# Block-diagonal k by DMA and patches turned by transposing DMAs, in a vision tower on one core

## The chip, the cores and the metric

The kernel runs on one core of one Trainium2 chip. A core has five engines that work through instruction streams of their own, in order: PE (TensorE, matmuls and transposes into the PSUM memory), DVE (VectorE), ACT (ScalarE), POOL (GpSimd) and SP (SyncE, which here only issues DMAs). They share the on-chip memory SBUF and wait for each other through semaphores. The metric is the device time of one execution in microseconds (us), the median of three runs.

## What is computed

Sixty-four images of 3 x 112 x 112 are cut into 49 patches of 768 values. With a class token in front each image has L = 50 tokens of 256 values.

```python
xn = _rms_norm(patches)
xq = _act_quant(xn)                     # 8-bit integers times a scale, per patch
h = concat([cls, xq @ wq.T], axis=1) + pos_embedding
for i in range(3):                      # three attentions; with 50 tokens all windows see the same tokens
    q, k, v = (proj(W, b) for W, b in ((Wq[i], bq[i]), (Wk[i], bk[i]), (Wv[i], bv[i])))   # 16 heads of 16
    scores = einsum('bhqd,bhkd->bhqk', q, k) * 4, causal
    w = e / (sum(e) + 1e-06)            # e = exp(scores - max)
    out_i = layer_norm(einsum('bhqk,bhkd->bhqd', w, v) @ Wo[i].T + bo[i])
h = h + layer_norm(concat(out_i) @ Wout.T + bout)      # input of the attentions: layernorm(h)
h = h + ffn(layernorm(h))               # quantized to 8 bits: silu(x @ Wg.T) * (x @ Wu.T), then @ Wd.T; width 704
```

## The kernel before

The 64 images go in eight groups (m) of eight; two images, 64 rows apart, make a pair that fills the 128 partitions, so a group has four pairs (p) and the kernel 32 pairs (n). The first program block does patches and attention for all groups, the second the feed-forward part. In the first, each engine walks its own list of steps. The table `AT` gives each step's places in its engine's list, sorted by `engine_order`; a step is a kind, a number within the group and the group. The lists of neighbouring groups are interleaved. So the order of the work is written out as numbers, and semaphores only keep it right.

The steps that matter here, per pair: "sums" (SP loads x_in, ACT and DVE gather the row statistics), "shift" (ACT scales into x_t, L733; DVE rounds into the bf16 buffer x_q, L1083), "turn_q" (PE turns x_q by six transposes of 128 columns into a PSUM bank, L1287; ACT copies the bank to x_qT, L746, or for a chunk of the feed-forward weights, which pass through the same steps as a ninth group, to wgT, L743), "embed" (PE multiplies x_qT by the token weights, L1296; DVE finishes the row, L1104), "norm_x" and "turn_x". Of x_t, x_q and x_qT there is one buffer each: DVE writes the next x_q when the last one has been turned and copied out.

Per group follow q and k for each of the three windows w and the two halves c of the 256 dimensions ("k" and "q": six matmuls each on PE, L1314; ACT evicts them to kT, L766, and qT), v (L1333), and then scores per step s (six in a group: window and half of the images). A score matmul (L1358) takes 64 partitions, the 16 dimensions of four heads, so k must stand block-diagonally in k_bd: for each head its own 16 rows, zeros elsewhere. Before the change POOL writes k_bd in "spread": it multiplies kT, repeated four times, by a mask of rows (L905, two operations of 128x400 per pair and window, 192 in all). k_bd has four slots of one pair each, so POOL waits until the scores of the slot's last user are through. After the scores: maximum and exponent ("max", "soft", "sum", "over" on DVE, ACT), POOL normalizes (L914), PE turns the probabilities ("turn_p", L1373), ACT copies them to pT (L806, L813), PE multiplies by v ("heads", L1383) and by the output weights ("project", L1394 and L1399), DVE accumulates.

All PE results except scores go through four PSUM banks in turn; `bank_plan` deals them out in the order of PE's list, and a step waits until its bank's last user has been evicted (`wait_released`). "fold" (L1253) and other set-up steps prepare weights during group 0.

Of the kernel before, what the change touches and what calls it, by code (L numbers as in the profile page):

```python
# [69 lines left out]
        "sums": (0, 1, 5, 6, 7, 8, 9, 10, 11, 12, 13, 14, 15, 16, 17, 18, 19, 20, 21, 22, 23, 24, 25, 26, 27, 28, 29,  # L70
            30, 31, 32, 33, 34, 35, 36, 37, 38, 39, 40,),
        "weights": (2, 3, 4,),
    },
    "act": {
        "sums": (0, 1, 10, 11, 25, 26, 51, 54, 99, 100, 117, 125, 176, 178, 195, 200, 250, 256, 268, 278, 324, 326,
            342, 346, 401, 402, 429, 439, 481, 482, 501, 504,),
        "shift": (2, 5, 13, 15, 33, 39, 61, 71, 106, 113, 137, 145, 185, 188, 205, 213, 260, 266, 283, 289, 332, 338,
            356, 362, 407, 419, 451, 466, 490, 495, 511, 528, 563, 568, 595, 618,),
        "tok_shift": (3,),
        "turn_q": (4, 9, 16, 19, 43, 55, 69, 82, 110, 129, 140, 156, 189, 209, 221, 232, 265, 277, 292, 298, 337,  # L80
            358, 367, 376, 421, 445, 460, 471, 496, 508, 527, 538, 577, 593, 611, 635,),
        "tok_copy": (6, 7,),
        "q_hi": (8,),
        "k_hi": (12,),
        "v_cut": (14, 18, 36,),
        "small": (17,),
        "wv_hi": (20,),
        "turn_x": (21, 22, 23, 24, 93, 95, 97, 98, 170, 171, 172, 173, 244, 246, 247, 248, 319, 321, 322, 323, 397,
# [1709 lines left out]
```

## Time and profile before

| | us |
|---|---|
| runs shown: median (lowest to highest) | 771.42 (769.8 to 774.2) |
| the profiled execution | 769.84 |
| its span, first to last instruction | 768.1 |
| PE busy | 684.5 (89%) |
| DVE busy | 641.9 (84%) |
| ACT busy | 584.3 (76%) |
| POOL busy | 520.0 (68%) |
| mean granted TensorE clock | 0.975 |

The span is the profiled execution's; 1.7 us lie around it. Busy time is the union of an engine's instructions; PE's matmuls overlap each other in the records, so a matmul's own duration is longer than its distance to the next. What a block of matmuls costs PE is read as the distance from its first start to the next block's first start. A timeline row gives start, length, engine, line, operation, and in brackets the engine's idle time ahead of it and what ended it.

### The profile page before, as it was taken

To read this page: it belongs to the slowest core of one execution; us is meant where nothing else is said; L and a number is where in the kernel's file an instruction comes from. 1 tells how busy PE (TensorE), PEld (TensorE's weight loads), DVE (VectorE), ACT (ScalarE), POOL (GpSimd) and SP (SyncE) were. 2 spreads that over 40 slices of the span, in tenths; PEclk is the share of its full clock that TensorE was granted. 3 is DMA by queue.
4 is the path that set the end of the run, shared out by engine and by line. 5 is a ranking of instruction groups with operands and counts; after the bars stand their busy time and mean duration, and the time that the engine had idled before them with its cause. 6 is when DMAs were issued, how large, how long until landed. Compare 5 with 4: busy or idle time off the path is not lost. (4 is left out here: it accounts for less than half of the span.)

```text
span 768.1 us, 25770 instructions
## 1 busy us (share of the span) xinstructions
PE 684.5 (89%) x9862; PEld 535.2 (70%) x9862; DVE 641.9 (84%) x1395; ACT 584.3 (76%) x1280; POOL 520.0 (68%) x793
## 2 busy tenths in 40 slices
PE   0498799999999999999999999999999999568866
PEld 0277678777877787877877787788778777334455
DVE  4788876899889988989898899889987898759947
ACT  3567888687788678869778878688868887379875
POOL 3459965957687859877677789478948786521154
PEclk9979999999999999999999999999999999869979
DMA  8301000000000000101000000100100000000005
GB/s 240 100 28 33 17 19 17 19 18 20 4 32 27 10 2 34 34 2 33 18 19 3 16 19 3 34 18 18 41 3 22 20 22 22 1 1 1 0 24 148
DMA packets 14980, 21.95 MB, mean 29 GB/s; under 512 B 1992, under 2 KB 11466, under 8 KB 14860
## 3 DMA queue, kind: packets, MB, share of 16 engines
q1 hardware_dynamic: 14424, 19.91, 8.4%
q8 instruction: 80, 1.31, 0.7%
q10 hardware_dynamic: 436, 0.40, 0.4%
q14 instruction: 40, 0.33, 0.1%
HBM read 17.03 MB, written 3.28 MB: 26 GB/s over the span
## 5 line engine op out<-in xcount | busy, mean ns | idle before, releaser
L905 POOL TENSOR_TENSOR k_bd<-kT,rmask 128x400 f32<-128x400 f32 x192 | 167.8, 902 | 7.5 <-PE ps_s L1358 4.3
L806 ACT COPY pT<-ps_w 25x400 f32<-25x400 f32 x192 | 94.8, 494 | 9.2 <-PE ps_w L1373 6.7
L1399 PE MATMUL ps_w<-oy_hi,o_hi 128*128 128x512 f32 x192 | 94.9, 494 | 0.0
L914 POOL TENSOR_TENSOR prob_hi<-prob_hi,rsum 128x800 f32<-128x800 f32 x48 | 74.9, 1559 | 13.3 <-DVE rsum L1151 13.3
L1134 DVE TENSOR_REDUCE nmax<-ps_s 128x16 f32<-128x400 f32 x96 | 72.4, 765 | 11.6 <-PE ps_s L1358 11.3
L786 ACT COPY v_bd<-ps_w 50x256 f32<-50x256 f32 x192 | 70.4, 367 | 13.2 <-PE ps_w L1333 10.9
L1399 PE MATMUL ps_w<-oy_hi,o_lo 128*128 128x512 f32 x192 | 76.3, 397 | 0.0
L1399 PE MATMUL ps_w<-oy_lo,o_hi 128*128 128x512 f32 x192 | 76.2, 397 | 0.0
L827 ACT ACTIVATE ps_w<-ps_w 128x256 f32<-128x256 f32 x96 | 35.6, 371 | 51.7 <-PE ps_w L1399 50.3
L1358 PE MATMUL ps_s<-k_bd,qT 64*25 64x200 f32 (+1 forms) x3072 | 70.5, 291 | 0.0
L919 POOL TENSOR_TENSOR ln<-ln,ln_eps 128x1 f32<-128x1 f32 x96 | 19.9, 208 | 74.6 <-ACT ps_w L827 74.1
L1314 PE MATMUL ps_w<-xh_dense,qk_hi 128*128 128x400 f32 x192 | 68.5, 357 | 1.5 <-DVE xl L1126 1.1
L1314 PE MATMUL ps_w<-xl,qk_hi 128*128 128x400 f32 x192 | 67.2, 350 | 0.0
L1314 PE MATMUL ps_w<-xh_dense,qk_lo 128*128 128x400 f32 x192 | 66.2, 345 | 0.0
L1333 PE MATMUL ps_w<-wv_hi,xh 128*128 128x256 f32 x192 | 61.9, 322 | 0.0
L921 POOL TENSOR_TENSOR ln<-ln,neg_half 128x1 f32<-128x1 f32 x96 | 54.4, 567 | 7.5
L914 POOL TENSOR_TENSOR prob_lo<-prob_lo,rsum 128x400 f32<-128x400 f32 x48 | 42.5, 886 | 19.5 <-DVE rsum L1151 19.5
L1373 PE MATMUL ps_w<-pack,prob_hi 128*128 128x128 f32 x384 | 51.7, 277 | 2.9 <-DVE acc L1169 1.0
L1333 PE MATMUL ps_w<-wv_lo,xh 128*128 128x256 f32 x192 | 54.0, 281 | 0.0
L1333 PE MATMUL ps_w<-wv_hi,xl 128*128 128x256 f32 x192 | 53.7, 280 | 0.0
L1373 PEld LDWEIGHTS ps_w<-pack,prob_hi 128*128 128x128 f32 x384 | 42.1, 141 | 11.1 <-issue 6.5
L813 ACT COPY pT<-ps_w 128x400 f32<-128x400 f32 x96 | 43.3, 506 | 8.1 <-PE ps_w L1373 7.3
(237 smaller groups left out, 2070.4 us busy)
## 6 DMA issues: line engine op xcount, KB each, us to landing
x_in<-in_x SPq DMA_DIRECT2D x64, 147.0 KB
out<-hidden SPq DMA_DIRECT2D x14, 200.0 KB
pT<-in_tok_w SPq DMA_DIRECT2D x1, 768.0 KB, 6.5
hidden<-in_wq SPq DMA_DIRECT2D x1, 768.0 KB, 8.6
k_bd<-in_wk SPq DMA_DIRECT2D x1, 768.0 KB, 9.5
v_bd<-in_wv SPq DMA_DIRECT2D x1, 768.0 KB, 9.2
hidden<-in_wout SPq DMA_DIRECT2D x1, 768.0 KB, 9.3
hidden<-in_wo SPq DMA_DIRECT2D x1, 768.0 KB, 10.8
```

Of the source, the lines that this page charges most:

```text
L786: last = nc.scalar.copy(v_bd[row:row + L, s % 2, b::2, :, e * HD:(e + 1) * HD], v_ps[src:src + L, :, e])
L806: last = nc.scalar.copy(pT[ROWB * h:ROWB * h + LQ, s % 2, c::2, :, 0:LQ], ps_w[row:row + LQ, bank].rearrange("p (j t) -> p j t", j=4)[:, : ...
L813: nc.scalar.copy(pT[:, s % 2, 4 * a:4 * a + 4, :, LQ:L], ps_w[:, bank].rearrange("p (j t) -> p j t", j=4)[:, :, 0:QB * LQ].rearrange("p j ...
L905: last = nc.gpsimd.tensor_tensor(k_bd[:, v % KBD, c], kT[:, w % 2, c, 2 * p * L:(2 * p + 2) * L].unsqueeze(1).broadcast_to([P, HR, 2 * L]) ...
L914: nc.gpsimd.tensor_tensor(pr, pr, rsum[:, s % 2, e].unsqueeze(2).broadcast_to([P, H, WIDTH[e]]), ALU.mult).then_inc(prob_ready, 1)
L921: nc.gpsimd.tensor_tensor(ln2[:, v, 2:3], ln2[:, v, 1:2], neg_half[:, 0:1], ALU.pow).then_inc(r2_ready, 1)
L1134: nc.vector.tensor_reduce(top, s_ps, AX.X, ALU.max, negate=True).then_inc(max_ready, 1)
L1314: mm = nc.tensor.matmul(G[:, 0:GT], wt[:, w, q, k, c * P:(c + 1) * P], xt[:, k, :, 0:L], start=(t == 0), stop=(t == 3 * KC - 1))
L1333: mm = nc.tensor.matmul(cols, xt[:, k, two].rearrange("p b t -> p (b t)"), wt[:, w, k], start=False, stop=(k == KC - 1 and xt is xl))
L1358: mm = nc.tensor.matmul(ps_s[32 * b:32 * b + LQ, e, r, c * HR * W:(c + 1) * HR * W], qT[rows, w % 2, c, first:first + LQ], k_bd[rows, v % ...
L1373: mm = nc.tensor.transpose(G[:, j * P:(j + 1) * P], flat[:, (4 * a + j) * P:(4 * a + j + 1) * P], pack[:])
L1399: mm = nc.tensor.matmul(G[:], ot[:, s % 2, c, 2 * (p % 2):2 * (p % 2) + 2].rearrange("p b t -> p (b t)"), wt[:, w, c], start=False, stop=( ...
```

## The change

Three things change.

First, k_bd is no longer computed by POOL but written by DMAs. The columns of the q and k weights are put into another order as they are split into high and low parts (`by_dim`, `in_dims`), so that partition 4i + h of a half holds dimension i of head h. Head h's rows are then every fourth partition, and the step "kbd" on SP copies them by one DMA per head, four per step s, from kT (now ordered by pair) into k_bd. The zeros are written once, by "kclear" on POOL. The scores wait for the landing (`kbd_landed`). The mask rmask goes, and the biases of q and k are loaded in the new order by sixteen DMAs ("biases") in place of two.

Second, from the second group on, and for the four weight chunks of gate and up, the patches are turned by the step "turn_d" on SP: six transposing DMAs of 128 x 128 from x_q to x_qT (or wgT). It waits for x_q and for the embed of the pair before; embed and the next x_q wait for its landing. PE's six transposes and ACT's copy stay for group 0 alone.

Third, the numbers in `AT` are new for all five engines; SP's list grows from 41 to 122 steps.

```diff
+        "kbd": (10, 11, 14, 15, 20, 23, 24, 25, 30, 31, 33, 34, 38, 39, 43, 44, 47, 48, 52, 53, 57, 58, 60, 65, 66,
...
+        "turn_d": (12, 17, 18, 21, 27, 29, 32, 36, 40, 45, 46, 50, 54, 59, 61, 62, 70, 73, 74, 79, 82, 83, 89, 90,
...
+        "turn_q": (5, 9, 17, 18,),
...
-    kT = sb(att, "kT", [P, 2, KC, GT])
+    kT = sb(att, "kT", [P, 2, PAIRS, KC, 2 * L])
...
-    SMALL = 16 * 12
+    SMALL = 16 * 9
...
+
+    def by_dim(t):
+        return t.rearrange("p (s k) (a h i) -> p s (k a) i h", k=KC, h=HR, i=HD)
+
+    def in_dims(t):
+        return t.rearrange("p s k (a i h) -> p s (k a) i h", h=HR, i=HD)
...
+                if kind == "turn_d":
+                    n = PAIRS + step[1]
+                    c = ffn_chunk(n // PAIRS, n % PAIRS)
+                    sp.wait_ge(xq_ready, n + 1)
+                    if c is None:
+                        bank, fill = bank_of(("embed", (n - 1) % PAIRS, (n - 1) // PAIRS))
+                        sp.wait_ge(filled[bank], fill)
+                        dst = x_qT[:]
+                    else:
+                        dst = wgT[:, c // 2, 3 * (c % 2):3 * (c % 2) + 3].rearrange("p f k t -> p (f k) t")
+                    for j in range(PC):
+                        sp.dma_start(dst[:, j], x_q[:, j * P:(j + 1) * P], transpose=True).then_inc(xqT_turned, 16)
                 if kind == "weights" and step[1] == 0:
-                    for dst, src in ((mask_st, mask), (hmask, head_mask), (qbias[:], bq), (kbias[:], bk), (gcol, ln_g),
+                    for dst, src in ((mask_st, mask), (gcol, ln_g),
...
+                if kind == "biases":
+                    for dst, src in ((qbias, bq), (kbias, bk)):
+                        for a in (0, 1):
+                            for h in range(HR):
+                                row = a * ROWB + h * HD
+                                sp.dma_start(dst[a * ROWB + h:(a + 1) * ROWB:HR], src[row:row + HD]).then_inc(loads["bias"], 16)
+                if kind == "kbd":
+                    s = step[1]
+                    w, q = s // 2, s % 2
+                    sp.wait_ge(k_ready, KC * (NS * m + w) + 2)
+                    if m == 0 and s == 0:
+                        sp.wait_ge(kbd_clear, 1)
+                    need(sp, scores_ready, (U * m + 2 * (s - 1) + AHEAD) if m > 0 or s > 1 else 0)
+                    for h in range(HR):
+                        sp.dma_start(k_bd[h::HR, 2 * q:2 * q + 2, :, h, :],
+                                     kT[h::HR, w % 2, 2 * q:2 * q + 2]).then_inc(kbd_landed[q], 16)
...
+            sp.wait_ge(xqT_turned, 16 * PC * PAIRS * GROUPS)
...
+                    act.wait_ge(loads["bias"], 16 * 16)
...
-                    nc.scalar.copy(qk_hi[:, :, 0], by_row(st_q)).then_inc(split_q, 1)
+                    nc.scalar.copy(in_dims(qk_hi[:, :, 0]), by_dim(st_q)).then_inc(split_q, 1)
...
-                    c = ffn_chunk(m, p)
-                    if c is not None:
-                        w_ps = ps_w[:, bank, 0:PC * P // 2].bitcast(BF16)
-                        dst = wgT[:, c // 2, 3 * (c % 2):3 * (c % 2) + 3].rearrange("p f k t -> p (f k t)")
-                        nc.scalar.copy(dst, w_ps).then_inc(xqT_ready, 1)
-                        return
...
-
-                    act.wait_ge(kbd_ready, V * m + (0, -PAIRS, PAIRS)[w] + AHEAD)
-                    nc.scalar.activation(kT[:, w % 2, c], ps_w[:, bank, 0:GT], ACT.Identity,
+                    for landed in kbd_landed:
+                        need(act, landed, 64 * (NS * m + (0, -1, 1)[w]))
+                    nc.scalar.activation(kT[:, w % 2, :, c], ps_w[:, bank, 0:GT].rearrange("p (v t) -> p v t", v=PAIRS), ACT.Identity,
                                          bias=kbias[:, w * KC + c:w * KC + c + 1]).then_inc(k_ready, 1)
...
+                if kind == "kclear":
+                    nc.gpsimd.memset(k_bd[:], 0.0).then_inc(kbd_clear, 1)
...
-                if kind == "spread":
-                    v = step[1]
-                    w, p = v // PAIRS, v % PAIRS
-                    pool.wait_ge(k_ready, KC * (NS * m + w) + 2)
-                    pool.wait_ge(consts, 1)
-                    pool.wait_ge(small_ready, 1)
-                    pool.wait_ge(scores_ready, U * m + 2 * ((v - KBD) // 2 + 1) + AHEAD)
-                    for c in range(KC):
-                        last = nc.gpsimd.tensor_tensor(
-                            k_bd[:, v % KBD, c], kT[:, w % 2, c, 2 * p * L:(2 * p + 2) * L].unsqueeze(1).broadcast_to([P, HR, 2 * L]),
-                            rmask[:].unsqueeze(2).broadcast_to([P, HR, 2 * L]), ALU.mult)
-                    last.then_inc(kbd_ready, 1)
...
-                    nc.vector.tensor_tensor(qk_lo[:, :, 0], by_row(st_q), qk_hi[:, :, 0].bitcast(F32), ALU.subtract).then_inc(qk_cut, 1)
+                    nc.vector.tensor_tensor(in_dims(qk_lo[:, :, 0]), by_dim(st_q), in_dims(qk_hi[:, :, 0]).bitcast(F32),
+                                            ALU.subtract).then_inc(qk_cut, 1)
...
-                    need(dve, xqT_ready, n)
+                    need(dve, xqT_ready, min(n, PAIRS))
+                    need(dve, xqT_turned, 16 * PC * (n - PAIRS))
                     nc.vector.tensor_scalar(x_q[:], x_t[:], MAGIC, None, ALU.subtract).then_inc(xq_ready, 1)
...
-                    pe.wait_ge(xqT_ready, PAIRS * m + p + 1)
+                    if m == 0:
+                        pe.wait_ge(xqT_ready, p + 1)
+                    else:
+                        pe.wait_ge(xqT_turned, 16 * PC * (PAIRS * (m - 1) + p + 1))
...
-                    pe.wait_ge(kbd_ready, V * m + 2 * s + 2 + AHEAD)
+                    pe.wait_ge(kbd_landed[q], 64 * (NS * m + w + 1))
```

PE in group 1, around the embeds of its first two pairs (tokT,x_qT); `ps_w<-hidden` are the folds of the output weights, `id,x_q` the transposes, `pack` the turned probabilities. Before:

```order
L1373 MATMUL ps_w<-pack,prob_lo 128x128 x4
L1296 MATMUL ps_w<-tokT,x_qT 128x256 x6
L1287 MATMUL ps_w<-id,x_q 128x128 x6
L1349 MATMUL ps_s<-mask,pick 128x200 x2
L1358 MATMUL ps_s<-k_bd,qT 25x100 x16
L1349 MATMUL ps_s<-mask,pick 128x8x25 x2
L1358 MATMUL ps_s<-k_bd,qT 25x200 x16
L1243 MATMUL ps_w<-id,hidden 128x128 x4
L1253 MATMUL ps_w<-hidden 128x256 x4
L1373 MATMUL ps_w<-pack,prob_hi 128x128 x8
L1243 MATMUL ps_w<-id,hidden 128x128 x4
L1296 MATMUL ps_w<-tokT,x_qT 128x256 x6
```

and after the change:

```order
L1320 MATMUL ps_w<-tokT,x_qT 128x256 x6
L1274 MATMUL ps_w<-hidden 128x256 x12
L1320 MATMUL ps_w<-tokT,x_qT 128x256 x6
L1397 MATMUL ps_w<-pack,prob_lo 128x128 x4
L1354 MATMUL ps_w<-bias,ones 128x256
```

The transposes between the embeds are gone, and the three folds alone stand between the two. (Each fold of the listing's x4 shows as x8 in the profile's records.)

PE in group 2 of the changed kernel, from its first pair's embed to its second's; `mask,pick` and `k_bd,qT` are scores, `pT,v_bd` heads:

```order
L1320 MATMUL ps_w<-tokT,x_qT 128x256 x6
L1397 MATMUL ps_w<-pack,prob_lo 128x128 x4
L1373 MATMUL ps_s<-mask,pick 128x200 x2
L1382 MATMUL ps_s<-k_bd,qT 25x100 x16
L1407 MATMUL ps_w<-pT,v_bd 32x50 x32
L1373 MATMUL ps_s<-mask,pick 128x8x25 x2
L1382 MATMUL ps_s<-k_bd,qT 25x200 x16
L1397 MATMUL ps_w<-pack,prob_hi 128x128 x8
L1320 MATMUL ps_w<-tokT,x_qT 128x256 x6
```

and around the first of these two embeds before the change:

```order
L1383 MATMUL ps_w<-pT,v_bd 32x50 x32
L1349 MATMUL ps_s<-mask,pick 128x200 x2
L1358 MATMUL ps_s<-k_bd,qT 25x100 x16
L1349 MATMUL ps_s<-mask,pick 128x8x25 x2
L1358 MATMUL ps_s<-k_bd,qT 25x200 x16
L1296 MATMUL ps_w<-tokT,x_qT 128x256 x6
L1373 MATMUL ps_w<-pack,prob_lo 128x128 x4
L1314 MATMUL ps_w<-xh_dense,qk_hi 128x400
```

The embeds of one group have moved closer to each other here: before, q and k matmuls, a transposing block and more stand between the two.

SP after the biases; before the change only the loads of x stand here:

```order
L616 DMA acc<-in_brow 1x1024
L631 DMA x_in<-in_x 49x768 x60
L628 DMA x_in<-in_w_gate 128x2x256
```

and after it:

```order
L640 DMA kbias<-in_bk 16x6 x8
L665 DMA x_in<-in_x 49x768 x4
L649 DMA k_bd<-kT 32x4x100 x8
L621 DMA_TRANSPOSE x_qT<-x_q 128x128 x6
L665 DMA x_in<-in_x 49x768 x2
L649 DMA k_bd<-kT 32x4x100 x8
L665 DMA x_in<-in_x 49x768 x2
L621 DMA_TRANSPOSE x_qT<-x_q 128x128 x12
```

SP's queue now holds three kinds of DMAs behind each other, each with a wait of its own in front.

## Rows read from the trace of the kernel before

**Rows 1.** The page's first part: busy us of each engine, share of span, instructions.
```profile
PE 684.5 (89%) x9862; PEld 535.2 (70%) x9862; DVE 641.9 (84%) x1395; ACT 584.3 (76%) x1280; POOL 520.0 (68%) x793
```

**Rows 2.** Table of windows: from:to, length, busy us per engine, PEclk, DMA share, GB/s.
```profile
40.00:80.00 40.00, 36.68 (x388) 29.15 (x386) 33.12 (x64) 29.52 (x56) 32.17 (x37) 0.92 0.08 24
80.00:640.00 560.00, 544.18 (x8660) 438.27 (x8658) 488.17 (x1103) 447.10 (x1023) 424.79 (x662) 1.00 0.06 19
```

**Rows 3.** Timeline of POOL, then of ACT: start us, us, what, [idle before, releaser].
```profile
53.60 9.89 POOL L905 TENSOR_TENSOR k_bd<-kT,rmask 128x400 f32<-128x400 f32 x8 [0.90 <-ACT kT L766]
...
63.58 0.60 ACT L766 ACTIVATE kT<-ps_w,kbias 128x400 f32<-128x400 f32 x1 [3.67 <-POOL k_bd L905]
```

**Rows 4.** Timeline of PE in the tail: the last attention heads.
```profile
658.58 0.92 PE L1383 MATMUL ps_w<-pT,v_bd 128*32 128x50 f32 x64 [2.27 <-ACT pT L813]
```

**Rows 5.** Timeline of PE around two blocks of turned patches (L1287).
```profile
62.06 0.49 PE L1287 MATMUL ps_w<-id,x_q 128*128 128x128 bf16 x6 [0.83 <-issue]
62.37 0.43 PE L1314 MATMUL ps_w<-xh_dense,qk_hi 128*128 128x400 f32 x1
...
63.56 0.28 PE L1330 MATMUL ps_w<-bias,ones 96*128 96x256 bf16 x1
...
132.19 0.51 PE L1287 MATMUL ps_w<-id,x_q 128*128 128x128 bf16 x6
132.63 0.26 PE L1349 MATMUL ps_s<-mask,pick 64*128 64x200 bf16 x2
```

**Rows 6.** Groups of instructions: xcount | busy us, mean ns of one | idle before, releasers.
```profile
L905 POOL TENSOR_TENSOR k_bd<-kT,rmask 128x400 f32<-128x400 f32 x192 | 167.8, 902 | 7.5 <-PE ps_s L1358 4.3 <-ACT kT L766 3.2
...
L746 ACT COPY x_qT<-ps_w 128x768 bf16<-128x768 bf16 x32 | 25.5, 797 | 4.8 <-DVE ln L1107 4.1 <-PE ps_w L1287 0.4
```

**Rows 7.** SP's timeline (issues); DMA issues (KB, us to landing); SP's waits (total, times, longest).
```profile
4.06 0.63 SPq L607 DMA_DIRECT2D hidden<-in_head_mask  x1
...
646.11 0.80 SPq L628 DMA_DIRECT2D x_in<-in_w_down  x2
...
id<-in_ident SPq DMA_DIRECT2D x1, 64.0 KB, 7.2
...
SPq L634 <- DMA x_in<-in_w_down: 2.0, 1, 2.0
```

**Rows 8.** Timeline of PE in groups 0 and 3: starts of one block after the other.
```profile
82.25 1.89 PE L1253 MATMUL ps_w<-hidden 128*128 128x256 f32 x8
84.07 0.69 PE L1269 MATMUL ps_w<-ybias,hidden 1*128 1x256 f32 x2
...
325.39 0.27 PE L1349 MATMUL ps_s<-mask,pick 64*128 64x200 bf16 x2
...
326.08 0.26 PE L1349 MATMUL ps_s<-mask,pick 64*128 64x200 bf16 x2
...
327.11 1.09 PE L1373 MATMUL ps_w<-pack,prob_hi 128*128 128x128 f32 x8
328.13 0.92 PE L1383 MATMUL ps_w<-pT,v_bd 128*32 128x50 f32 x64
328.98 0.66 PE L1373 MATMUL ps_w<-pack,prob_lo 128*128 128x128 f32 x4
329.55 1.09 PE L1373 MATMUL ps_w<-pack,prob_hi 128*128 128x128 f32 x8
330.95 0.27 PE L1330 MATMUL ps_w<-bias,ones 96*128 96x256 bf16 x1 [0.31 <-DVE o_lo L1158]
...
331.78 0.28 PE L1330 MATMUL ps_w<-bias,ones 96*128 96x256 bf16 x1
...
332.62 0.39 PE L1394 MATMUL ps_w<-bias,ones 96*128 96x512 bf16 x1
...
334.25 0.83 PE L1296 MATMUL ps_w<-tokT,x_qT 128*128 128x256 bf16 x6
334.92 0.38 PE L1394 MATMUL ps_w<-bias,ones 96*128 96x512 bf16 x1
```

More of the change, by code:

```diff
@@ new lines @@
+        "embed": (4, 5, 7, 8, 19, 39, 40, 41, 58, 69, 78, 83, 103, 119, 120, 121, 144, 167, 168, 171, 186, 205, 211,
+            212, 242, 243, 246, 252, 278, 291, 295, 302,),
+        "k_lo": (6,),
+        "kclear": (9,),
+        "v_left": (10, 11,),
+        "z_left": (12, 27,),
+        "clear": (15, 16, 17, 18,),
+        "sum": (20, 21, 23, 25, 31, 32, 33, 38, 46, 47, 48, 49, 53, 56, 57, 62, 66, 74, 75, 77, 82, 87, 88, 89, 90,
[4 rows of a table added]
+        "turn_x": (22, 28, 29, 30, 59, 60, 61, 71, 114, 138, 143, 149, 150, 164, 165, 169, 192, 193, 209, 238, 244,
+            256, 265, 269, 280, 284, 292, 296, 311, 314, 322, 330,),
@@ new lines @@
+        "sum": (47, 56, 57, 63, 76, 77, 81, 89, 101, 123, 125, 127, 141, 143, 150, 155, 167, 178, 179, 188, 200, 217,
[4 rows of a table added]
+        "over": (53, 59, 61, 64, 82, 83, 84, 93, 102, 124, 126, 133, 144, 151, 153, 156, 169, 181, 186, 189, 203,
[4 rows of a table added]
+        "fold_lo": (55, 58, 60,),
+        "o_lo": (75,),
+        "heads": (79, 80, 103, 105, 137, 159, 165, 187, 199, 201, 240, 250, 271, 274, 289, 300, 342, 344, 371, 376,
+            394, 395, 438, 451, 460, 477, 492, 493, 531, 543, 573, 574, 590, 596, 632, 645, 665, 681, 682, 695, 726,
+            730, 753, 768, 780, 787, 794, 804,),
@@ L248 @@
[L248 to L253 removed]
[4 rows of a table removed]
+        "turn_x": (12, 13, 15, 16, 75, 77, 78, 79, 142, 144, 146, 147, 214, 215, 216, 218, 278, 279, 283, 284, 345,
+            347, 350, 351, 416, 417, 418, 420, 485, 487, 488, 490,),
@@ new lines @@
+        "wo_turn": (26, 32, 33,),
+        "scores": (28, 30, 31, 34, 46, 47, 50, 53, 63, 66, 74, 76, 90, 91, 95, 97, 108, 109, 115, 124, 125, 133, 143,
[4 rows of a table added]
+        "fold": (37, 38, 39,),
+        "turn_p": (41, 45, 48, 49, 62, 65, 67, 68, 87, 92, 94, 98, 106, 110, 114, 122, 126, 131, 132, 134, 154, 160,
[7 rows of a table added]
+        "y_spread": (52,),
+        "heads": (54, 55, 70, 71, 96, 107, 113, 128, 137, 138, 166, 172, 188, 189, 200, 211, 236, 237, 258, 259, 273,
+            274, 303, 309, 317, 328, 342, 343, 367, 375, 395, 396, 409, 411, 438, 447, 460, 470, 471, 483, 507, 508,
+            525, 531, 540, 547, 551, 559,),
@@ L264 @@
     "mix": PAIRS, "mix2": PAIRS, "k": NS * KC, "q": NS * KC, "v": S, "heads": S, "spread": V, "project": V,
-    "scores": U, "max": U, "soft": U, "sum": U, "over": U, "turn_p": U,
+    "kbd": S, "scores": U, "max": U, "soft": U, "sum": U, "over": U, "turn_p": U,
 }
@@ L375, in layer @@
     b_mean = sb(att, "b_mean", [1, NS])
[L378 removed]
+    gcol, bcol, o_mean, bo_col, tok_sum = (hidden[:, 7, 8 * j:8 * j + n] for j, n in enumerate((6, 6, 6, 6, 4)))
     st_out, st_o, st_q = (hidden[:, 8 + 6 * j:14 + 6 * j] for j in range(3))
@@ L394, in layer @@
     y_in = ybias[0:1]
-    loads = {n: sem("l_" + n) for n in ("ident", "small", "tok", "wq", "wk", "wv", "wo", "wout", "rows_v", "rows")}
+    loads = {n: sem("l_" + n) for n in ("ident", "small", "bias", "tok", "wq", "wk", "wv", "wo", "wout", "rows_v", "rows")}
     x_clear = sem("x_clear")
```

191 lines of the change are left out of this document (82 added, 109 removed), and 133 rows, old and new, of the table AT.

## The prediction

> **What bounds the kernel now.** I read the page first: PE is busy 89% of the span, DVE 84%, ACT 76%, POOL 68% [rows 1]. A share of the whole span mixes stages, so the table of windows comes next. From 80 to 640 us, while all eight groups go through attention, PE is busy 544.18 of 560 us at a granted clock of 1.00; DVE has 488, ACT 447, POOL 425 [rows 2]. PE idles 15.8 us there, under 3%. In that stretch the kernel is as long as PE's list of matmuls, and work taken from another engine gives nothing by itself. Ahead of it, from 40 to 80 us, PE idles 3.3 of 40 us, and POOL is the late one: it writes k_bd for 9.89 us on end, and ACT's next kT waits 3.67 us for it [rows 3]. After 640 us comes a tail with little beside it [rows 4], then the feed-forward block, which the change touches only in who turns four weight chunks, all ahead of it.
>
> **What goes from PE.** Before, each pair (or weight chunk) has six bf16 transposes on PE. PE is in order and back to back, so a block costs the distance from its start to the next block's: 62.06 to 62.37 and 132.19 to 132.63, that is 0.31 to 0.44 us [rows 5]. Of 36 blocks 4 stay and 32 go: 32 x 0.38 = **12.2 us**, all of it on the path. ACT loses the copies that emptied them: 28 x 0.797 and four of weights, some 25 us; POOL loses 192 x 0.902, the page's 167.8 us [rows 6]. Neither engine bounds, so both count at nothing on their own, only through PE's waits.
>
> **What gets smoother.** The 15.8 us of PE's idle time from 80 to 640 us [rows 2] are many short waits for evictions, softmax and statistics. POOL is without its largest job, ACT 25 us lighter, and all orders are remade, so some of it goes: at most all 15.8; at the other end the new orders are worse and it grows. I take a third, **5.3 us**. In the tail PE stops 2.27 us for ACT between the last transposes of the probabilities and the last heads [rows 4]; the new order has one projection block (1.6 us [rows 8]) in that hole: **1.6 us**.
>
> **What the transposing DMAs cost.** No row shows one. Pair n's six may be issued when x_q(n) is written and PE is through embed(n-1) (x_qT is one buffer), and embed(n) waits for their landing. So between two embeds PE must have other work for T = six issues + landing. The nearest rows: SP issues a plain DMA in 0.40 us (two in 0.80) to 0.63, and the block's last one was still awaited 2.0 us once issued [rows 7]. Low: 6 x 0.40 + 2.0 = 4.4. High: the identity, 64 KB over the same 128 rows, took 7.2 us to land among other loads [rows 7], so 6 x 0.63 + 7.2 = 11.0. I take 6 x 0.63 + 2.0 = 5.8, say 6: in this stretch the DMA engines are 6% busy [rows 2], unlike when the identity came in.
>
> What stands between embeds in the new order I price by rows, start to next start [rows 8]: scores 0.69 and 1.03, transposed probabilities 1.02 and (the short ones) 0.57, heads 0.85, v 0.84 for each half, projection 1.63, embed 0.67, a fold 1.82, six k or q matmuls 1.19 [rows 5]. For the second pair of group 1 only the three folds are there: 5.4 us. For the second pair of group 2: 0.57 + 0.69 + 0.85 + 1.03 + 1.02 = 4.2 us. The other short gaps, priced so, are 6.3, 6.8, 7.4, 7.6, 8.1, 8.2, 8.5, 9.4 and 9.8; the rest are over 11. The stall is the sum of T minus gap wherever that is positive: 0.2 us at T = 4.4, 0.6 + 1.8 = **2.4** at 6, 10.3 at 8, 18 at 9, 28 at 10, 39 at 11. x_q is one buffer too: DVE's next x_q waits for the same landing, and behind it on DVE are softmax steps that PE needs. Priced the same way, at least 6.8 us of PE work lie between the embed and that point of DVE's order, so up to T = 6 this adds nothing.
>
> Six transposes on PE cost 0.31 to 0.44 us together [rows 5]. The Trainium skill, page "VectorE: DVE Perf Modes", section "The three transpose paths", gives one 128x128 bf16 transpose 390 ns on TensorE and 1309 ns on the DMA's crossbar, and prefers TensorE where PSUM will do as destination. By its figure six in a row make T an estimated 6 x 1.31 + 2.0 = 9.9 us, and the sum would end slower than before. The trace does not bear out its TensorE figure for transposes issued back to back; no run here shows the other.
>
> **What the DMAs of k cost.** A step of k was four POOL operations, 4 x 0.902 = 3.6 us [rows 6]; it is four DMAs and a landing, 4 x 0.40 + 2.0 to 4 x 0.63 + 2.0, that is 3.6 to 4.5 us [rows 7]. The shortest distance on PE from the last k matmul to the scores that need the step is 5.6 us (first window of group 3), the other groups' 5.9 to 7.7, later steps at least 6.6. With ACT's copy of kT in between that is covered, if barely: nothing; a landing as slow as the identity's would cost up to 5 us in each of eight groups. SP works in order, so a transposing step that waits for an embed holds back the k steps behind it; but a group's first k step needs that group's embeds itself, so it never stands behind one that is still open. Clearing k_bd on POOL falls where POOL has 7.8 of 40 us free [rows 2], ahead of the first k: nothing. Sixteen bias loads replace two, 16 x 0.40 to 16 x 0.63 = 6 to 10 us of SP between 20 and 30 us, over before the first kT at about 50: nothing; without that cover up to 10 us, once.
>
> **Sum.** Against the profiled execution's own 769.84 us: -12.2 - 1.6 - 5.3 + 2.4 = -16.7, so 753.1. The median of the runs is 771.42, 1.6 above, so 754.7, say **755 us**.
>
> **Rivals.** (a) **Slow transposes; slower than before.** Without smoothing the gain is 13.8 (PE's work and the tail). At T = 9 the stalls of 18 us exceed it: 771.4 - 13.8 + 18 = 776. T = 10 gives 786, T = 11 gives 797; it decides from T = 8.5 on. For it: the identity's 7.2 us, and that no row shows such a DMA. Against: six independent transfers on engines that are 94% idle. 0.14; and 0.04 for a time beyond all this, if every two-byte element became a packet. The Trainium skill's 1309 ns, named above, is a case of (a). (b) **The gain handed back.** At T = 8 the stalls are 10.3 and nothing gets smoother: 771.4 - 13.8 + 10.3 = 768, down to 762 with less of either. The relief of POOL, the largest item of the change, is then worth nothing. For it: POOL and ACT never bounded from 80 to 640 us [rows 2], and a chain that took PE 0.4 and ACT 0.8 us now takes T. 0.16, half of it too small to measure. (c) **Much smoother.** POOL was the late one from 53 to 63 us [rows 3]; if its queue is also behind most of the later short waits, 12 of the 15.8 us go and 2 at the start: 771.4 - 13.8 - 14 + 2.4 = 746. Against: PE is 97% busy there already. 0.08.
>
> **How the numbers follow.** Forecast 755 (749 to 761): 0.58; (b) 762 to 771: 0.16; (c): 0.08; (a) 0.14 and 0.04. About 0.5%, 3.9 us, is what a measurement of this kernel can tell from no change. Faster: 0.58 + 0.08 + 0.08 = 0.74; same 0.08; slower 0.18. The range 745 to 776 holds the forecast, (b) and (c), 0.82, and takes in T from 4.4 to 9.
>
> **What would show it.** In the changed kernel's profile: 192 transposes fewer on PE; POOL near 350 us busy; PE's idle time through the groups near 13 us. If embed's matmuls wait for a DMA by more than a few us in total, T is over 6; issue and landing of x_qT<-x_q give T itself. If scores wait for k_bd's DMA, the k path is too long. The prediction is wrong if T is 9 or more, or if SP is so taken up with issuing that loads of x come late.

## The result, and the profile after

| | before | after |
|---|---|---|
| median (lowest to highest) | 770.79 (769.8 to 774.2) | 912.16 (908.83 to 918.17) |
| ratio, 95% interval | | 1.183 (1.175 to 1.192) |
| profiled execution, its span | 769.84, 768.1 | 908.83, 907.0 |
| mean granted TensorE clock | 0.975 | 0.899 |

The changed kernel is 18% slower. The median before is of four runs here; 771.42 was that of three. I had forecast 755, and my range ended at 776. The page of the changed kernel first: busy time by engine and the granted clock in 40 slices. They answer to [rows 1].

```profile
PE 716.8 (79%) x9670; PEld 554.3 (61%) x9670; DVE 633.4 (70%) x1394; ACT 565.9 (62%) x1248; POOL 358.7 (40%) x602
...
PEclk9878888889988798998989989999989987978979
```

POOL has 161 us less to do, as planned, and PE 192 transposes less. PE's share fell from 89% to 79% all the same, and its clock line, which read 9 in almost every slice before, has 8s all along. The next view is the window in which all groups are in attention, against [rows 2]; the columns are length, busy us of the engines (PE, PEld, DVE, ACT, POOL), granted clock, share of the DMA engines and GB/s.

```profile
80.00:640.00 560.00, 468.42 (x6789) 371.18 (x6790) 386.77 (x897) 344.62 (x802) 218.20 (x382) 0.90 0.15 38
```

PE was busy 544 of 560 us before, now 468, and at a clock of 0.90 in place of 1.00. What it waits for stands in the view of waits (engine, tile and line, released by; us in total, times, longest):

```profile
PE ps_w L1320 <- DMA x_qT<-x_q: 67.3, 19, 6.5
...
DVE x_q L1104 <- DMA x_qT<-x_q: 61.0, 13, 7.9
...
DVE hidden L1125 <- PE ps_w L1320: 31.8, 15, 5.6
PE ps_s L1373 <- issue: 31.4, 8, 8.3
```

PE waits 67 us for the patches turned by DMA, DVE 61 us for the same landings before it may write the next x_q, and 31 us go before score matmuls, put down to "issue". The timeline shows why the first is so long. SP's queue and PE around the first two turned pairs (start, length, engine, line, operation, in brackets the idle time ahead and its releaser):

```profile
71.50 7.59 SPq L621 DMA_TRANSPOSE x_qT<-x_q  x6
79.14 0.82 SPq L665 DMA_DIRECT2D x_in<-in_x  x2
80.06 5.18 SPq L649 DMA_DIRECT2D k_bd<-kT  x8
...
86.22 7.75 SPq L621 DMA_TRANSPOSE x_qT<-x_q  x6
```

```profile
80.30 1.46 PE L1320 MATMUL ps_w<-tokT,x_qT 128*128 128x256 bf16 x6 [3.73 <-DMA x_qT<-x_q]
...
95.17 1.46 PE L1320 MATMUL ps_w<-tokT,x_qT 128*128 128x256 bf16 x6 [6.06 <-DMA x_qT<-x_q]
```

Six transposing DMAs take SP 7.6 us to issue; 1.2 us after the last one's issue is over the embed starts. Over the 19 embeds that waited, the median from the first issue to the embed is 9.6 us. That is T, which I had taken as 6. The issue of the six has a median of 8.4 us there (7.5 to 8.9).

**Where the time went.** The last projection of the attention block ends at 665.8 us before and at 803.4 after; the feed-forward part behind it is 1.3 us longer (103.6 us, 102.3 before). To split these +137.6 us I walked PE's list of steps in the trace and gave each step (transposes of patches apart) the mean distance to the next step that it has in the trace of before. The list holds the steps of the groups; PE's set-up of the weights, the folds among it, some 19 us in all, is left out. So the list is 581.8 us long in both kernels; the work done by 80 us, the transposes and the idle time after 80 us come from the traces, and "slower" is what is left: matmuls that take longer than before. Most of the experiments are in the same table, as differences from the kernel before:

| kernel | end of attention | work behind at 80 us | transposes | PE idle after 80 us | slower matmuls |
|---|---|---|---|---|---|
| after | +137.6 | +9.8 | -11.7 | +100.6 | +39.0 |
| kbd_on_pool | +101.9 | +9.8 | -11.7 | +73.7 | +30.1 |
| two_buffers | +120.4 | +9.8 | -11.7 | +90.4 | +31.9 |
| sp_by_ready | +119.2 | +9.8 | -11.7 | +86.2 | +35.0 |
| both_old_orders | +88.5 | +3.5 | -11.7 | +71.3 | +25.3 |
| turns_only | +78.2 | +2.7 | -11.7 | +55.1 | +32.2 |
| plain_turns | +36.0 | +8.9 | -11.7 | +30.7 | +8.1 |
| old_one_big | +14.7 | +0.9 | -11.7 | +16.4 | +9.0 |
| one_big | +1.8 | +8.9 | -11.7 | +3.1 | +1.4 |
| selective | -0.3 | +0.9 | -5.9 | +1.1 | +3.6 |
| k_only | -1.3 | +0.9 | 0 | -2.9 | +0.6 |
| hyb62 | -10.2 | +4.7 | -11.7 | +0.9 | -4.0 |

The last column holds the scatter between single executions too, some 5 us either way. "Behind at 80 us" reads too high, and "slower" too low, for a kernel that runs the folds earlier: the three folds start at 78.1, 82.3 and 84.7 us in the kernel before and run from 70.9 to 76.2 in hyb62. Counted with them, hyb62 is level with the kernel before at 80 us, and its -4.0 becomes about +1.

### The profile page after: what moved, and what is told of

Same layout as the page of the kernel before. It is cut to its first block and busy times, and to the rows that moved or that the text cites. A ratio compares the mean times of both kernels' runs of the same rounds, so it can differ in the third digit from the quotient of the medians.

```text
span 907.0 us, 25378 instructions
## 1 busy us (share of the span) xinstructions
PE 716.8 (79%) x9670; PEld 554.3 (61%) x9670; DVE 633.4 (70%) x1394; ACT 565.9 (62%) x1248; POOL 358.7 (40%) x602
## 5 line engine op out<-in xcount | busy, mean ns | idle before, releaser
L1423 PE MATMUL ps_w<-oy_hi,o_hi 128*128 128x512 f32 x192 | 100.2, 522 | 0.0
L1320 PE MATMUL ps_w<-tokT,x_qT 128*128 128x256 bf16 x192 | 38.6, 359 | 70.6 <-DMA x_qT<-x_q 67.3
L1423 PE MATMUL ps_w<-oy_hi,o_lo 128*128 128x512 f32 x192 | 79.4, 414 | 0.0
L1423 PE MATMUL ps_w<-oy_lo,o_hi 128*128 128x512 f32 x192 | 79.4, 414 | 0.0
L1104 DVE TENSOR_SCALAR x_q<-x_t 128x768 bf16<-128x768 f32 x36 | 25.9, 719 | 75.3 <-DMA x_qT<-x_q 61.0
L1382 PE MATMUL ps_s<-k_bd,qT 64*25 64x200 f32 (+1 forms) x3072 | 76.2, 309 | 2.1 <-issue 2.1
L1338 PE MATMUL ps_w<-xh_dense,qk_hi 128*128 128x400 f32 x192 | 70.6, 368 | 4.9 <-DVE acc L1190 4.9
L1320 PEld LDWEIGHTS ps_w<-tokT,x_qT 128*128 128x128 bf16 x192 | 20.8, 122 | 83.5 <-DMA x_qT<-x_q 72.9
L1397 PE MATMUL ps_w<-pack,prob_hi 128*128 128x128 f32 x384 | 54.7, 289 | 2.7 <-DVE acc L1190 1.1
```

What stands on the lines that cost most here:

```text
L1320: mm = nc.tensor.matmul(G[:, 0:D], x_qT[:, c], tokT[:, c], start=(c == 0), stop=(c == PC - 1))
L1338: mm = nc.tensor.matmul(G[:, 0:GT], wt[:, w, q, k, c * P:(c + 1) * P], xt[:, k, :, 0:L], start=(t == 0), stop=(t == 3 * KC - 1))
L1382: mm = nc.tensor.matmul(ps_s[32 * b:32 * b + LQ, e, r, c * HR * W:(c + 1) * HR * W], qT[rows, w % 2, c, first:first + LQ], k_bd[rows, v % ...
L1397: mm = nc.tensor.transpose(G[:, j * P:(j + 1) * P], flat[:, (4 * a + j) * P:(4 * a + j + 1) * P], pack[:])
L1423: mm = nc.tensor.matmul(G[:], ot[:, s % 2, c, 2 * (p % 2):2 * (p % 2) + 2].rearrange("p b t -> p (b t)"), wt[:, w, c], start=False, stop=( ...
```

## The experiments

Ratios are to the kernel before, run on the same chip beside each, with 95% intervals.

| kernel | median us | ratio |
|---|---|---|
| plain_turns | 805.93 | 1.047 (1.042 to 1.051) |
| k_only | 764.05 | 0.992 (0.989 to 0.995) |
| turns_only | 846.41 | 1.100 (1.095 to 1.104) |
| both_old_orders | 861.60 | 1.119 (1.114 to 1.124) |
| two_buffers | 891.29 | 1.154 (1.150 to 1.158) |
| kbd_on_pool | 877.05 | 1.134 (1.130 to 1.138) |
| filler | 900.58 | 1.166 (1.162 to 1.171) |
| selective | 769.85 | 0.996 (0.994 to 0.999) |
| one_big | 770.70 | 0.998 (0.995 to 1.001) |
| old_one_big | 781.92 | 1.013 (1.010 to 1.016) |
| sp_by_ready | 891.73 | 1.157 (1.153 to 1.161) |
| one_big_pieces | 767.81 | 0.994 (0.991 to 0.997) |
| k_only_pieces | 764.44 | 0.990 (0.987 to 0.993) |
| hyb78 | 770.40 | 0.997 (0.995 to 0.9995) |
| hyb62 | 763.97 | 0.990 (0.985 to 0.994) |

### Which part of the change costs

**plain_turns**: the six DMAs without the transposition.

```diff
-    sp.dma_start(dst[:, j], x_q[:, j * P:(j + 1) * P], transpose=True).then_inc(xqT_turned, 16)
+    sp.dma_start(dst[:, j], x_q[:, j * P:(j + 1) * P]).then_inc(xqT_turned, 16)
```

> The changed kernel, with its six transposing DMAs per pair written as plain DMAs of the same 128x128 blocks (same queue, same waits, same orders). The patches and the gate and up weights are not turned: the turning itself is left out of the computation. Theory 1 (the cost of the transposing form is what went wrong: in the trace of the changed kernel six are 1.27 us apart, so T is 9.7 us where I took 6): issue falls to 0.3 to 0.6 us each, T to about 5, and the time to 755 to 775. Theory 2 (SP works in order, and k's DMAs and the loads of x wait behind steps that wait for x_q, whatever the six DMAs cost): stays at 830 or more. Theory 3 (the new orders are bad in themselves): stays at 800 or more with PE waiting for other things than x_qT and k_bd.

Measured 805.93. Six plain DMAs take SP 0.60 us each and T is 5.6 us. So 106 of the 141 us hang on the transposing form. But 35 us remain at a T that is *under* the 6 us of my forecast: none of the three theories alone (embeds and scores still stop PE for 18.6 and 16.0 us), and the stalls that I had summed for a given T were wrong as well as T.

**k_only**, the first part alone: the diff of k_bd with the old table of orders; only SP's list is new.

> The first part of the change alone: k_bd by DMAs, with the orders of the kernel before (only SP's list is new, k's steps placed where POOL's were ready in the trace of before); all patches turned by PE and ACT as before. Theory 1: k's DMAs cost nothing and POOL's relief brings little, 762 to 772. Theory 2 (issue and landing of k's DMAs are on the path of every group's scores): 790 or more, with scores waiting for k_bd.

Measured 764.05, theory 1: k's DMAs cost nothing here, and taking 160 us from POOL brings 5.7 us. The page's table of DMAs (tile, queue, operation, count, size, median us from issue to landing):

```profile
k_bd<-kT SPq DMA_DIRECT2D x192, 50.0 KB, 1.9
```

**turns_only** (transposing DMAs, POOL's k_bd, old orders) and **both_old_orders** (both parts, old orders):

```diff
-        "turn_q": 36 places in the lists of PE and ACT
+        "turn_q": the 4 of group 0
+        SP: "turn_d" where x_q and the embed before were ready in the trace
```

> The second part of the change alone: transposing DMAs from the second group on, k_bd by POOL, the orders of the kernel before (PE's and ACT's steps of turning taken out). Priced on the trace of before, a T of 9.7 us from x_q or the last embed to the next embed exceeds the room there by 42 us in sum, and 12 us of PE's transposes go. Theory 1 (the chain of transposes is too long): 800 to 850. Theory 2 (only together with k's DMAs on one queue is it slow): 760 to 785.

> Both parts of the change with the orders of the kernel before; SP's list made from the times at which each step was ready in the trace of before. Theory 1 (transposes): as turns_only, within 10 us. Theory 2 (one queue for both): 30 us or more above turns_only. Theory 3 (the new orders are bad in themselves): well under the changed kernel's 912, below 850; if the new orders help, above 912.

Measured 846.41 and 861.60. The transposes alone cost 77 us in orders made for PE's transposes: theory 1. Both together cost 15 us more than the transposes alone, where k_only by itself gained 6: so 21 us come up only where both are in. SP's queue is what they share; that it is the queue is argued here; in the new orders kbd_on_pool, below, shows it. 861.60 is in the range of none of its three theories. From there to the changed kernel it is another 50 us (861.6 to 912.2): the new orders with T this long, and in them SP's list, which in both_old_orders goes by readiness (sp_by_ready, below, gets 20 us from that alone).

### What makes T long

In the trace of the changed kernel each transposing DMA is 1.23 us on SP, and its packets (128 of 256 bytes) all start within 0.25 us, 1.2 us after its issue; then nothing moves until the next one's. So the DMA engines are idle most of T. **one_big** gives the same job to one instruction:

```diff
-    for j in range(PC):
-        sp.dma_start(dst[:, j], x_q[:, j * P:(j + 1) * P], transpose=True).then_inc(xqT_turned, 16)
+    sp.dma_start(dst, x_q[:], transpose=True).then_inc(xqT_turned, 16)
```

> The changed kernel with one transposing DMA of 128 x 768 per pair in place of six of 128 x 128; same result, orders and waits. In the trace of the changed kernel the 128 packets of each transposing DMA move within 0.25 us, 1.2 us after its issue, and then nothing moves for 1.0 us until the next one's. Theory 1 (the 1.23 us is a cost of each instruction on SP): T falls to some 3 to 4 us, as short as PE's way, and the time to between 755 and 805 (plain_turns, T of 5.6, had 806). Theory 2 (the transposing itself takes 1.2 us for 128 columns wherever it is issued): T stays at 8 or more and the time within 15 us of 912.

Measured 770.70, within the noise of the kernel before: 141 us come back by one edit. The two rows of SP that answer to 7.59 and 7.75 above, and the landing in the view of DMAs:

```profile
72.35 1.36 SPq L620 DMA_TRANSPOSE x_qT<-x_q  x1
...
80.84 1.24 SPq L620 DMA_TRANSPOSE x_qT<-x_q  x1
```

```profile
x_qT<-x_q SPq DMA_TRANSPOSE x28, 2.9
```

One transposing DMA takes SP 1.24 us whether it has 128 or 768 columns, and lands 2.9 us after its issue. The six were slow as six instructions, not as data. Theory 2 falls.

**old_one_big**: the same edit in both_old_orders.

> Both parts of the change with the orders of the kernel before and one transposing DMA of 128 x 768 per pair. By theory 1 of one_big, T of 3 to 4 us leaves stalls of 1 to 5 us in these orders and PE saves 12 us against k_only's 764: 752 to 762, and it would beat the kernel before and k_only. By theory 2 it stays near both_old_orders, 850 or more.

Measured 781.92, not the 752 to 762 of theory 1. PE idles 16 us more than before: 8 us at embeds (two stops of 4.0 and 3.4 at the first pair of a group), the rest in small waits. The orders made for PE's way of turning leave 2.4 and 3.0 us between x_q and these two embeds, which a T of 3.9 and 5.6 us overruns. Here the new orders are better by 11 us.

### The single buffers, and SP's queue

**two_buffers**: x_q and x_qT twice, by parity of the pair.

```diff
+    q_buf = (x_q[:], wg_flat[:, 3 * DIN:4 * DIN])
+    qT_buf = (x_qT[:], wg_flat[:, 2 * DIN:3 * DIN].rearrange("p (c t) -> p c t", c=PC))
-    nc.vector.tensor_scalar(x_q[:], x_t[:], MAGIC, None, ALU.subtract)
+    nc.vector.tensor_scalar(q_buf[buf(n)], x_t[:], MAGIC, None, ALU.subtract)
```

> The changed kernel with two buffers each of x_q and x_qT from the third group on (the second ones lie in the part of wgT that is empty until the last weight chunks); orders, queues and the six transposing DMAs as they are. Theory 1 (it is the chain through the single buffers, x_q to landing to embed and to the next x_q, that stops PE and DVE): most of the 67 us for which embeds wait and of DVE's 61 go, 800 to 840. Rival (SP itself, 7.6 us for each pair and everything behind it, is what stops the others): 880 or more.

Measured 891.29: DVE's wait for x_qT's landing falls from 61 to 11 us, but embeds still stop PE for 62 us (67 in the changed kernel). The time is in the rival's range: 21 us come back, and the single buffers were not what stops PE at most embeds. In its trace x_q(16) is written at 337.8 us, its six are issued from 339.9 to 348.0, behind eight k_bd DMAs, and the embed starts at 349.2 after 5.7 us of idle time; x_q(15) is ready at 294.9 but its six are issued from 302.8, behind the six of pair 14 (to 296.5), eight k_bd DMAs and two of x. The chain is T plus SP's queue, from an x_q that comes late on DVE.

**kbd_on_pool**: k's 192 DMAs issued by POOL.

```diff
-    sp.dma_start(k_bd[h::HR, 2 * q:2 * q + 2, :, h, :], kT[h::HR, w % 2, 2 * q:2 * q + 2])
+    pool.dma_start(k_bd[h::HR, 2 * q:2 * q + 2, :, h, :], kT[h::HR, w % 2, 2 * q:2 * q + 2])
```

> The changed kernel with k's 192 DMAs issued by POOL instead of SP, each step where it was ready in the trace of the changed kernel. Theory 1 (k's steps stand behind transposing steps on SP, and scores wait 33 us for it): scores' waits go and the time falls by 30 to 50, to 860 to 880, if POOL's issue is not slower than SP's. Rival (k's DMAs are not on the path, their waits only follow from embeds that come late): within 10 us of 912. If POOL's own issue costs over 1.5 us each, its list becomes late and the run tells little.

Measured 877.05, theory 1: 35 us come back. PE's idle time ahead of scores falls from 32.8 to 8.2 us, at embeds from 67.3 to 41.5 (turning steps no longer stand behind k's); 19 us come up ahead of transposed probabilities, since POOL's own steps now stand behind k's. The same is read from the changed kernel's trace: for eight of the 19 embeds that waited, SP began to issue the six 2.1 to 5.4 us after x_q was written and the embed before had ended, since k's DMAs and loads of x stood in front. Counted up to the length of each wait this is 27 of the 67 us. The plainest case of such a queue is in the changed kernel's last group. SP, then PE, then ACT:

```profile
743.39 8.32 SPq L621 DMA_TRANSPOSE wgT<-x_q  x6
751.81 5.19 SPq L649 DMA_DIRECT2D k_bd<-kT  x8
```

```profile
755.84 0.35 PE L1373 MATMUL ps_s<-mask,pick 64*128 64x200 bf16 x2 [8.29 <-issue]
```

```profile
738.10 0.59 ACT L796 ACTIVATE kT<-ps_w,kbias 128x400 f32<-128x400 f32 x1 [1.30 <-PE ps_w L1338]
740.10 0.59 ACT L796 ACTIVATE kT<-ps_w,kbias 128x400 f32<-128x400 f32 x1 [1.41 <-PE ps_w L1338]
```

kT is written at 740.7 us. k's step is issued at 751.8, behind a weight chunk's six that nobody needs until the feed-forward block, and PE stops 8.29 us for it. These are the waits that the view of waits calls "issue".

**sp_by_ready**: SP's list sorted by readiness, everything still on SP.

> The changed kernel with SP's list alone in another order: its steps by the times at which their waits ended in the trace of kbd_on_pool, so that k's steps stand less behind transposing steps that are not ready. Six transposing DMAs per pair, everything on SP. Theory 1 (the places in SP's list cost, not that they share a queue): PE's waits for k_bd fall from 33 us to under 12 and the time to 870 to 885. Rival (as long as a transposing step holds SP for 7.6 us, no order helps): 900 or more.

Measured 891.73, between the two ranges: waits for scores fall to 17 us, not under 12, embeds stay at 64. An order of SP's list gives back 20 of the 35 us that a second queue gives back.

### What idle time does to the clock

Each wait of PE costs more than its length. The changed kernel around an embed that waited 6.3 us, PE's rows and then the windows (columns as above; the clock is the number behind POOL's busy time):

```profile
535.30 1.46 PE L1320 MATMUL ps_w<-tokT,x_qT 128*128 128x256 bf16 x6 [6.29 <-DMA x_qT<-x_q]
536.70 1.56 PE L1407 MATMUL ps_w<-pT,v_bd 128*32 128x50 f32 x64
```

```profile
528.00:535.30 7.30, 1.01 (x8) 0.77 (x9) 2.56 (x4) 2.25 (x4) 1.84 (x3) 0.85 0.11 23
535.30:540.00 4.70, 4.70 (x100) 3.41 (x108) 2.42 (x7) 1.67 (x4) 0.00 (x0) 0.50 0.08 17
540.00:544.00 4.00, 4.00 (x76) 3.37 (x60) 4.00 (x8) 3.32 (x8) 2.38 (x2) 1.00 0.09 17
```

The embed's six matmuls take 1.46 us, where they take 0.83 elsewhere in the same trace; the block of heads behind it is 1.56 us long, where it is 0.92 in the kernel before [rows 8]. From 535.3 to 540.0 the granted clock is 0.50, the lower of the two levels (1.2 GHz), from 540 on 1.00 again. The window ahead of it has 0.85: the clock had fallen while PE was still idle. Of the 28 embeds from the second group on, 13 run wholly at the low level in the changed kernel, and none before. This is the column of slower matmuls, 39 us: 0.26 to 0.58 us for every us of added idle time in the slow kernels of the table, mostly about 0.4.

**filler** puts work into these waits:

```diff
+    for c in range(PC * FILL.get(PAIRS * m + p, 0)):
+        nc.tensor.matmul(G[:, 0:D], tokT[:, c % PC, 0:P], tokT[:, c % PC], start=True, stop=True)
     pe.wait_ge(xqT_turned, 16 * PC * (PAIRS * (m - 1) + p + 1))
```

> The changed kernel with 456 matmuls added on PE whose result is overwritten, in front of the 19 embeds that waited for x_qT in its trace, each about 85% of that wait (51 us of work in all). Theory (PE's granted clock falls when PE idles, 0.90 against 1.00 before, and this costs some 49 us of matmul time on top of the idle 119): the clock rises to 0.94 or more and the time falls by 15 to 35 us although work was added. Rival (the clock is low for another reason, or costs nothing on the path): 912 or more.

Measured 900.58: 51 us of work added, 11.6 us faster. The window from 80 to 640 us has a clock of 0.95 in place of 0.90. The direction is the theory's, the size is short of its 15 to 35: PE's idle time fell by 41 us and the added work took 51, and the other matmuls got some 20 us faster. So about half of the 39 us is shown to be bought back by keeping PE busy; that the rest is the clock too is read from rows, not shown by a run.

### Where T is short: what is left

**selective**: transposing (in six) only where the trace of k_only has room.

> k_only (k_bd by DMAs, orders of the kernel before) with transposing DMAs for only the 11 pairs and the 4 weight chunks where the trace of k_only leaves at least 10.5 us from x_q or the last embed to the embed, and 10 to the next x_q. If T of 9.7 us is the whole of the cost of a transposing step, none of them stalls and PE saves 15 x 0.38 = 5.7 us: 764 - 5.7 = 758 (755 to 763). If they also cost by what stands behind them on SP: 765 or more.

Measured 769.85, against k_only's 764.05, each beside its own runs of before: 0.996 (0.994 to 0.999) to 0.992 (0.989 to 0.995). The 5.9 us of PE's transposes are saved and none of these embeds stops for long (2.8 us in all), and yet the time does not fall. Against k_only's trace there are 4.0 us more of small waits and 3.0 us of slower matmuls in their place. That fits what was expected if these steps also cost by what stands behind them on SP, but the trace does not single it out.

one_big still has 11.7 us of transposes less than the kernel before and is not faster. Its row in the table says where they are: 8.9 us of work are behind at 80 us already. The first k matmul starts at 59.0 us against 50.4. POOL and DVE of the changed kernel there:

```profile
35.08 4.18 POOL L898 TENSOR_TENSOR qk_lo<-k_bd,qk_hi 128x1536 fp32r<-128x1536 f32 x1
...
51.20 2.77 POOL L895 MEMSET k_bd<- 128x3200 f32 x1
```

```profile
35.53 4.14 DVE L1104 TENSOR_SCALAR x_q<-x_t 128x768 bf16<-128x768 f32 x1 [1.32 <-ACT x_t L769]
...
42.05 0.54 DVE L1104 TENSOR_SCALAR x_q<-x_t 128x768 bf16<-128x768 f32 x1
...
50.19 0.38 DVE L1139 TENSOR_SCALAR x_t<-hidden,ln 128x256 f32<-128x256 f32 x1
...
51.29 2.82 DVE L1139 TENSOR_SCALAR x_t<-hidden,ln 128x256 f32<-128x256 f32 x1
```

x_q takes 0.54 us, and 4.14 beside POOL's operation on k's weights; x_t takes 0.38 us, and 2.82 beside the clearing of k_bd, which I had costed at nothing. They end 0.4 and 0.1 us after POOL's operation. **one_big_pieces** and **k_only_pieces** cut these two:

```diff
-    nc.gpsimd.memset(k_bd[:], 0.0).then_inc(kbd_clear, 1)
+    for v in range(KBD):
+        for c in range(KC):
+            last = nc.gpsimd.memset(k_bd[:, v, c], 0.0)
+    last.then_inc(kbd_clear, 1)
```

> one_big with two operations of POOL cut into pieces: the clearing of k_bd (one memset of 128x3200, 2.77 us) into 8, and the low part of k's weights (128x1536, 4.18 us) into 6. In the traces of the changed kernel and of one_big, DVE's x_q beside the latter took 4.14 us in place of 0.54, and x_t beside the former 2.82 in place of 0.38; both start 0.1 to 0.5 us after POOL's operation and end 0.03 us before to 0.1 us after it. Theory 1 (DVE is held until POOL's operation ends, and these 6 us are on the path to the first k, which comes 9 us later than in the kernel before): 771 falls by 3 to 6, to 765 to 768. Rival (other things are late there, or DVE gets no turn between pieces): 769 to 772.

> k_only with the same two operations of POOL in pieces. In its trace the three x_t beside the memset took 3.67 us where they take about 1.1. Theory 1: 1 to 3 us under k_only's 764, 761 to 763. Rival: 764 or more.

In one_big_pieces, DVE's same operations:

```profile
34.62 0.80 DVE L1109 TENSOR_SCALAR x_q<-x_t 128x768 bf16<-128x768 f32 x1 [1.32 <-ACT x_t L768]
...
47.85 0.86 DVE L1144 TENSOR_SCALAR x_t<-hidden,ln 128x256 f32<-128x256 f32 x1
```

DVE is held by POOL's operation, and gets its turn between pieces: shown by 4.14 to 0.80 and 2.82 to 0.86. The first k comes at 53.0 in place of 59.0. The kernel gains less, 770.70 to 767.81, in the range of theory 1 but with intervals that overlap (0.995 to 1.001, 0.991 to 0.997). In its trace the folds run earlier too (from 75.4 us on, from 79.4 in one_big); counted with them, it is 4 us behind the kernel before at 80 us, and one_big 9. How much of that is in the medians these runs can't tell. k_only_pieces has 764.44, ratio 0.990 (0.987 to 0.993) against 0.992 (0.989 to 0.995) of k_only: no difference that these runs can tell.

**hyb78** and **hyb62**: one_big_pieces with the orders of k_only up to 78 or 62 us of its trace.

```diff
+    ORDERS = {engine: [steps of k_only that start before 62 us] + [the other steps as in one_big] ...}
```

> The orders of k_only for the steps up to 78 us of its trace, then those of the changed kernel; one transposing DMA of 128 x 768 per pair from pair 6 on; the two operations of POOL in pieces. Counted in PE's steps without the transposes, one_big stands 9 us behind the kernel before at 80 us and no further behind later. Theory 1 (the new orders lose their gain in the first 80 us alone): 756 to 762, better than both kernels. Rival (what the start loses is made up later anyway, by waits that then appear): 764 to 772.

> As hyb78, with the orders of k_only only up to 62 us. Theory 1: within 3 us of hyb78. If the orders between 62 and 78 us matter as much: 3 us or more above it.

Measured 770.40 and 763.97. hyb78 is the rival's: at 80 us its work, counted as in the table, is level with k_only's, and by 100 us it is 5.7 us behind (33.3 against 39.0), in waits where the two orders meet. hyb62 has the gain: 1.0% under before (0.6 to 1.5%), as fast as k_only_pieces. That is 6.4 us under hyb78, which neither expectation for it had, and its interval overlaps that of one_big_pieces (0.991 to 0.997). So a good start-up and a short T together bring out the transposes' 12 us only in part, and nothing I ran is more than about 1% faster than the kernel before. The new orders with PE still turning the patches were not run, so what these orders are worth by themselves stays open.

## Why the prediction was wrong, point by point

- **What bounds the kernel** [rows 1, 2]: right. PE's list is the length of the kernel, and POOL's relief is worth little: k_only takes 160 us from POOL and gains 5.7 us.
- **What goes from PE, -12.2**: right, 11.7 us after 80 us by the walk through the list.
- **T, "I take 6 x 0.63 + 2.0 = 5.8"**: the step that failed. I took the issue of a plain DMA for that of a transposing one; it is 1.23 us, twice my upper bound of 0.63, so 7.5 to 8.9 us of issue and T = 9.6. The upper end, 11.0, held it only because of a landing that did not occur (1.2 us after the last issue ended). "Six independent transfers on engines that are 94% idle" was the argument against: the engines were idle, and it did not matter, since SP issues one after another. The estimate of 9.9 us that I had worked out from the Trainium skill's 1309 ns ("VectorE: DVE Perf Modes", "The three transpose paths") was near; the trace of the changed kernel bears the figure out with a median of 1.28 us from one to the next. Part of it is luck: the issue of six was longer than the estimate's 7.9 us (8.4) and the landing shorter than its 2.0 (1.2). one_big shows that the price is per instruction, not per 128 columns.
- **The stalls for a given T**: the second step that failed, by omission. "The sum of T minus gap" counts from the embed before. By it T = 9.6 gives some 24 us; the nine embeds whose x_q was written by about the end of the embed before stopped PE for 23.1 us. The sum agrees, in part by luck: 7 of these us are late issue by SP, which the sum did not have. And T starts at the later of the embed and x_q, and in ten pairs (4, 8, 14, 16, 18, 20, 24, 26, 28, 30) x_q came 8 to 36 us after the embed before: 44.2 us, of which I had nothing (20 of them are late issue by SP again). "At least 6.8 us of PE work lie between" was read for the next x_q, not for the distance from x_q to its own embed. plain_turns shows the same at T = 5.6: 18.6 us at embeds where I had forecast under 2.4.
- **"A group's first k step never stands behind one that is still open"**: it held, and it was not enough. None of the eight waits put down to "issue" is at a group's first k step; they are at k steps of the second and third windows, which stood behind transposing steps: 31 us of PE's idle time. I had let "later steps at least 6.6" us of distance cover them. With k's DMAs on a queue of their own 35 us of kernel time come back (kbd_on_pool), by these waits and by turning steps that stood behind k's.
- **The granted clock**: missing. I priced a wait at its length. 39 us of slower matmuls, half of them shown to be the clock (filler).
- **Clearing k_bd, "nothing"**: wrong, 2.4 us, and 3.6 us by the other operation of POOL, which I had not looked at because the kernel before has it too, only not beside x_q. The Trainium skill, "SBUF — State Buffer", section "SBUF: two separate sides", has DVE and GpSimd share a port pair that one of them holds for a whole instruction. The rows agree: 4.14 for 0.54.
- **What gets smoother, -5.3, and the tail, -1.6**: not seen. With T short, idle time is 3.1 us more than before, not 5.3 less.
- **k's DMAs, biases**: right in themselves: landing 1.9 us, k_only not slower; the bias DMAs take SP 10.1 us, the upper bound that I gave.
- **The rivals**: (a) was the one that came, and it too was far too small: 786 for T = 10 where 912 came, for want of the three terms above (44 at embeds, 31 at scores, 39 by slower matmuls) and of the 10 us that are behind at 80 us. The 0.04 for a time beyond (a) had another reason, packets of two bytes; the transposing DMAs' packets have 256.

## What to carry to other kernels

Before a step goes to a DMA queue, count its instructions: here each transposing DMA held the queue for 1.24 us whether it moved 128 or 768 columns, so six cost 141 us of kernel time that one did not. A new latency starts at the *last* of its inputs and must be laid against the distance from each of them to the first reader; and everything issued from that queue afterwards is a reader as well. On a kernel that is all PE, price a wait of PE at some 1.4 times its length, an estimate from the last two columns of the table above.

## What the runs showed of the hardware that I had not expected

- A transposing DMA of 128x128 bf16 is 1.23 us on SP, of 128x768 1.24 us; a plain one of 128x128 0.60, one of 32 partitions x 400 floats 0.605, one of x 0.31 (median). All 128 packets of a 128x128 transposition start within 0.25 us.
- After 6.3 us of idle time PE's granted clock was 0.50 for the next 4.7 us of work, then 1.00.
- DVE's x_q took 4.14 us in place of 0.54 beside a POOL operation of 4.18 us, and 0.80 when that was cut into six.
- Splitting the weights with their columns in another order took ACT 2.8 us in place of 1.48 (two such), DVE 2.7 in k_only in place of 1.7 (4.13 in the changed kernel, where POOL works beside it), POOL 4.18 in place of 3.42.
- The same 192 DMAs of k_bd took POOL 0.55 us each to issue, SP 0.605.
